# A graph network on one core: in the message pass, the cap goes from GpSimd to VectorE, the product of gate and softplus from VectorE to GpSimd, and scaling and caps one iteration ahead

## The chip, the cores and the metric

The kernel runs on one core of a Trainium2 chip. The metric is the device time of one execution in microseconds. Five engines work side by side from their own instruction queues and meet through semaphores: TensorE (PE in the profile, its weight loads PEld), VectorE (DVE), ScalarE (ACT), GpSimd (POOL) and SyncE (SP), which here issues DMA transfers.

## The reference

Four graph network layers over 6250 nodes of 64 features and 200000 edges sorted by destination, each followed by a residual sum and a layer norm. The change lies in the third layer, in the part that turns every edge's 128 sums into a message of 64 features and sums the messages by destination:

```python
total = jnp.concatenate([atom_fea[dst], atom_fea[src], edge_fea], axis=1)
total = _batchnorm(total @ fc_w.T + fc_b, bn1_w, bn1_b)
gate, core = jnp.split(total, 2, axis=1)
messages = jax.nn.sigmoid(gate) * jax.nn.softplus(core)
aggr = jax.ops.segment_sum(messages, dst, num_segments=N)
```

## The kernel before

The edges are cut into two halves that lie in the lower and the upper 64 partitions, so that a block of 512 columns holds 1024 edges. There are 196 blocks; an iteration handles U = 4 of them, and a pass over the edges has 49 iterations. The kernel has seven passes in turn (SOFT, GCN1, GCN2, STAT, MSG, PNA1, PNA2). The statistics pass (STAT) has left every block's sums in memory (`total_d`, gate part and core part, 512 KB a block) and the scale `bnsc` and bias `bnbi` of the batch norm in columns. The message pass (MSG) reads them back and does the rest. It runs as `message_turns`: iteration after iteration, with a body for even and one for odd iterations (`par` is 0 or 1, and picks one of two sets of four buffers in `totals`, `acts` and `scaled`).

For block u of iteration i the work before the change is:

- SyncE, `message_moves(i)`: `total_load` (L445) brings the sums of block (i, u) into `totals`; it waits until iteration i-2 is through with that buffer, which means the sigmoid of ScalarE (the wait at L442) and GpSimd's two operations. Behind two loads in the same queue stand two stores `rows_store` (L434) of blocks three iterations back, and a small load of the mask (`mask_load`, L423).
- GpSimd, `scale_cores`: `acts` becomes min(core x scale, cap), L655, where the column `bncap` is CAP - bias; `scaled` becomes core x scale + bias, L656. It may be up to two iterations ahead.
- ScalarE, `gates` (sigmoid of the gate part, L1162), `exps` (exp with the bias added, L1170), `logs` (ln(1 + .), L1176), each over two blocks at once, and `rows_out` (L1127), which copies the transposed running sums of iteration i-1 out of PSUM into one of four slots of `obuf`. `rows_out` of a slot waits for the store that last emptied it. Sigmoid needs another function table than exp and ln, so that a table is loaded (L1162 and L1184) twice in every two iterations.
- VectorE, `message_sums`: `softplus` (L1526) is the larger of `acts` and `scaled`, into `msg`; `message` (L1532) multiplies `msg` by the gate; `message_scan` (L1514) is the running sum along the edges, restarted by the mask that TensorE has spread over PSUM (`spread_mask`, L852).
- TensorE, `turn_back` (L827): four transposes of the running sums, for `rows_out`.

The queue of ScalarE is written out by hand in `message_functions`. In the order of its lines, with 0 for blocks 0 and 1, and 2 for blocks 2 and 3, an odd iteration does gates 0, rows_out 0, gates 2, table, exps 0, rows_out 1, exps 2, logs 0, rows_out 2, logs 2, rows_out 3. An even one does exps 0, rows_out 0, exps 2, logs 0, rows_out 1, logs 2, table, gates 0, rows_out 2, gates 2, rows_out 3. The `rows_out` in iteration i are those of iteration i-1. `message_sums` issues softplus 0, message 0, and then for each u softplus u+1, scan u, message u+1.

Of the kernel before, what the change touches and what calls it, by code (L numbers as in the profile page):

```python
# [18 lines left out]
P = 128  # L19
# [4 lines left out]
BLK = P * J  # L24
U = 4
# [68 lines left out]
def gnn_kernel(nc, x, src, dst, ea128, ea16, ea64, W0, b0, W1, b1, W2, b2, fcw, fcb, bn1w, bn1b,  # L94
# [15 lines left out]
    with ctx:  # L110
# [86 lines left out]
        aT = expd  # L197
        stats = feat[:, :, :].rearrange("p w c -> p (w c)")[:, 0:2 * NB * 6].rearrange("p (n k) -> p n k", k=6)
        agg2 = sb("agg2", [P, 2])
        bnsc, bnbi, bncap = sb("bnsc", [P, 2]), sb("bnbi", [P, 2]), sb("bncap", [P, 1])  # L200
        nrow = sb("nrow", [P, 4, F])
        col1 = sb("col1", [P, 4])

# [35 lines left out]
        s_neg = ring("s_neg", one((SOFT, *PNA)))  # L239
        s_eT = ring("s_eT", one((STAT, *PNA)))  # L240
        s_eC = ring("s_eC", one((STAT, *PNA)))
        s_col = ring("s_col", {**one(GATHER), MSG: 2})
        s_zero_out = sem("s_zero_out")
        s_sed = ring("s_sed", one((STAT,), 32))
        s_seT = ring("s_seT", one((STAT,)))
# [1 line left out]
        s_hot = ring("s_hot", one((SOFT,)))  # L247
        s_hus = ring("s_hus", one((SOFT,)))
        s_top = ring("s_top", one((SOFT, MSG)))
        s_arg = ring("s_arg", one((SOFT,)))  # L250
        s_dec = ring("s_dec", one((SOFT, MSG)))
        s_exp = ring("s_exp", {SOFT: 1, MSG: 2})
        s_sg = ring("s_sg", one((MSG,)))
# [86 lines left out]
        def total_here(engine, i, par, u):  # L340

            if par:
                engine.wait_ge(s_sed.sems[u], i * 8 + (8 + s_sed.base[MSG]))
            else:
                engine.wait_ge(s_tot0[u], i * 8 + 16)
# [256 lines left out]
        def _(g):  # L602
# [41 lines left out]
                                             in_offset=bass.IndirectOffsetOnAxis(ap=idx, axis=0))\  # L644
                         .then_inc(s_gat.sems[u], 16)

            def scale_cores(i, par):

                for u in range(U):
                    total_here(g, i, par, u)  # L650
                    if not (isinstance(i, int) and i < 2):
                        s_cus.done(g, MSG, i - 2, u)
                    g.sem_inc(s_in_order, 1)
                    of = totals[:, par * U + u, BLK:]
                    g.tensor_scalar(acts[:, par * U + u, BLK:], of, bnsc[:, 1:2], bncap[:, 0:1], ALU.mult, ALU.min).then_inc(s_col.sems[u], 1)  # L655
                    g.tensor_scalar(scaled[:, par * U + u, :], of, bnsc[:, 1:2], bnbi[:, 1:2], ALU.mult, ALU.add).then_inc(s_col.sems[u], 1)  # L656

            def near_edges():

# [31 lines left out]
            for p in range(7):  # L691
                if p in GCN:
                    x_ = GCN.index(p)
                    if p == GCN1:
                        near_edges()
                    for m in range((MT - ROWS_LAG) * (1 - x_), MT):
                        local_rows(x_, m)
                    joint_rows(x_)
                    continue
                if p == MSG:  # L700
                    g.wait_ge(s_wc, 3)
                    message_turns(g, scale_cores)
                else:
                    if p == STAT:

                        g.wait_ge(s_zero_out, (2 * NB + 1) * 16)
                        for w in range(NT):
                            if w in FIRST_TILES:
                                g.wait_ge(s_tb, ENDS.index(GCN2) * Q + FIRST_TILES.index(w) + 1)
                            g.indirect_dma_start(out=seed_d, out_offset=bass.IndirectOffsetOnAxis(ap=starti[:, w:w + 1], axis=0),  # L710
                                                 in_=feat[:, w, 2 * F:4 * F], in_offset=None,
                                                 bounds_check=2 * H - 1, oob_is_err=False).then_inc(s_sc, 16)
                    if p != SOFT:
                        g.wait_ge(s_td, TABLE[p])
                    if p == STAT:

                        g.wait_ge(s_mi, 16)
                        g.indirect_dma_start(out=mid_row[:, :], out_offset=None, in_=tdst_d,
                                             in_offset=bass.IndirectOffsetOnAxis(ap=mid_i[:, 0:1], axis=0)).then_inc(s_mid, 16)
                    for u in range(U):  # L720
                        rows(p, 0, u)
                    with g.Fori(1, IT) as i:
                        for u in range(U):
                            rows(p, i, u)
                if p == STAT:
                    continue

                g.wait_ge(s_end, 1)
                s_out.all_done(g, p)
                if p > 0:  # L730
                    g.wait_ge(s_free, ENDS.index(p))
                r, k = (runs3_d, 3) if p in RUNS else (runs1_d, 1)
                for w in range(NT):
                    g.indirect_dma_start(out=feat[:, w, F:F + k * F], out_offset=None, in_=r,  # L734
                                         in_offset=bass.IndirectOffsetOnAxis(ap=endi[:, w:w + 1], axis=0))\
                     .then_inc(s_endg[sum(w >= z for _, z in SPAN)], 16)
# [371 lines left out]
        def _(act):  # L1108
# [56 lines left out]
            def exps(i, par, v):  # L1165

                for u in (v, v + 1):
                    s_col.part_done(act, MSG, i, u, 1)
                both = slice(par * U + v, par * U + v + 2)
                A(acts[:, both, BLK:], acts[:, both, BLK:], ACT.Exp, bias=bnbi[:, 1:2]).then_inc(s_exp.sems[v], 1)  # L1170

            def logs(i, par, v):

# [245 lines left out]
        def _(dve):  # L1419
# [105 lines left out]
                s_col.done(dve, MSG, i, u)  # L1525
                TT(msg[:, u, :], acts[:, par * U + u, BLK:], scaled[:, par * U + u, :], ALU.max).then_inc(s_top.sems[u], 1)  # L1526

            def message(i, par, u):

                s_sg.done(dve, MSG, i, u - u % 2)  # L1530
                s_top.done(dve, MSG, i, u)
                TT(msg[:, u, :], msg[:, u, :], acts[:, par * U + u, 0:BLK], ALU.mult).then_inc(s_cus.sems[u], 1)  # L1532

            def message_scan(i, u):

# [5 lines left out]

            def message_sums(i, par):

                softplus(i, par, 0)
                message(i, par, 0)
                for u in range(U):
                    if u + 1 < U:
                        softplus(i, par, u + 1)
                    message_scan(i, u)
                    if u + 1 < U:  # L1550
                        message(i, par, u + 1)

            def running_max(i, u):

# [96 lines left out]
            def edge_pass(p):  # L1651
                link(V.memset(res[:, 1, :, BLK:BLK + 1], 0.0))
                if p in GATHER and p != SOFT:
                    for u in range(U):
                        copy_indices(p, 0, u, u)
                if p == MSG:
                    message_turns(dve, message_sums)
                    return
                if p == SOFT:
                    link(V.memset(top[:, U - 1, BLK:BLK + 1], 0.0))  # L1660
                    s_col.done(dve, SOFT, 0, 0)
                    running_max(0, 0)
                    weights(0, 0)
                for u in range(U):
                    step(p, 0, u, False)
                with dve.Fori(1, IT - 1) as i:
                    for u in range(U):
                        step(p, i, u, False)
                for u in range(U):
                    step(p, IT - 1, u, True)  # L1670
# [408 lines left out]
            link(TT(bnsc[:, :], bnw_c[:, :], col1[:, 0:2], ALU.mult))  # L2079
            link(TT(bnbi[:, :], bnsc[:, :], nrow[:, 0, 0:4:2], ALU.mult))  # L2080
            link(TT(bnbi[:, :], bnb_c[:, :], bnbi[:, :], ALU.subtract))
            link(TS(bncap[:, :], bnbi[:, 1:2], -1.0, CAP, ALU.mult, ALU.add))
            dve.sem_inc(s_wc, 1)


# [113 lines left out]
```

## Time and profile before

| What | us |
|---|---|
| Median of 3 runs | 10464.34 (10455.72 to 10467.83) |
| The profiled execution's own time | 10463.46 |
| Its span in the profile | 10461.7 |
| Message pass, first GpSimd operation to last running sum | 5407.7 to 6037.2 |
| Busy in the whole span: PE, PEld | 5526.5 (53%), 4458.8 (43%) |
| Busy in the whole span: DVE, ACT, POOL | 6467.0 (62%), 2109.5 (20%), 7267.2 (69%) |

Busy times are sums over all seven passes, whose limits differ; the message pass takes some 630 of the 10462 us. The lines quoted further down are of that pass, and times in them count from the start of the span.

### The profile page before, as it was taken

How to read it: one execution, taken by the hardware profiler on the slowest of the kernel's cores; microseconds unless marked ns; L12 is line 12 of the kernel's file. 1: busy time of each engine (PE TensorE's matmuls, PEld its weight loads, DVE VectorE, ACT ScalarE, POOL GpSimd, SP SyncE). 2: the span in 40 equal slices, each digit the busy share in tenths (PEclk: the TensorE clock that was granted, in tenths of full speed). 3: DMA queues.
4: the chain of work that ended last, by engine and by line, in shares of the span. 5: the costliest groups of instructions: out<-in, count | busy, mean ns of one | idle time of the engine just before them, and what ended most of it. 6: DMA issues, size and time to landing. Idle time of an engine off the chain costs nothing.

```text
span 10461.7 us, 124350 instructions
## 1 busy us (share of the span) xinstructions
PE 5526.5 (53%) x33901; PEld 4458.8 (43%) x33999; DVE 6467.0 (62%) x8938; ACT 2109.5 (20%) x2960; POOL 7267.2 (69%) x7048
## 2 busy tenths in 40 slices
PE   4665666548887666666655523333333433333333
PEld 3444444347777445545432223333333333333333
DVE  6777777789932455555568855555555555555556
ACT  1111111137710011111127711111111111111111
POOL 6777777626612777777779947777777577777774
PEclk8777777769998788888865555656565665656556
DMA  8777777624477677777767715555555355555553
GB/s 184 195 195 195 196 196 196 159 83 188 190 282 267 226 238 237 235 239 235 235 209 246 253 49 124 124 125 124 125 123 125 80 124 124 124 124 124 124 124 76
DMA packets 2347313, 1784.12 MB, mean 171 GB/s; under 512 B 1805829, under 2 KB 1977610, under 8 KB 2342282
## 3 DMA queue, kind: packets, MB, share of 16 engines
q1 hardware_dynamic: 828055, 930.52, 27.0%
q10 hardware_dynamic: 1303632, 566.52, 20.3%
q0 software_dynamic: 215456, 284.72, 11.8%
q8 instruction: 119, 1.95, 0.1%
q14 instruction: 51, 0.42, 0.0%
HBM read 921.34 MB, written 861.11 MB: 170 GB/s over the span
## 4 chain that ended last, share of the span: by engine, by line
POOL 57%; issue 23%; DVE 7%; PE 5%; DMA 3%; ACT 2%; SPq 1%; POOLq 0%; ACTq 0%; DVEq 0%
POOL arena L643 53%; PE ph L968 2%; POOL feat L734 1%; POOL sum_d L679 1%; PE pn L968 1%; POOL arena L670 1%; DMA runs_d<-obuf 1%; DVE work L1514 1%; DMA arena<-in_x_dram,idx_src 1%; ACT arena L1170 1%; ACT arena L1176 1%; DVE obuf L1978 0%; PE pn L907 0%; DVE arena L1574 0%; DVE work L1526 0%
## 5 line engine op out<-in xcount | busy, mean ns | idle before, releaser
L643 POOL DMA_INDIRECT arena<-table_d,idx_src x3136 | 2983.0, 951 | 1117.9 <-issue 955.3
L806 PE MATMUL pn<-work,wblk 128*128 128x128 f32 x3136 | 1048.7, 438 | 2412.5 <-DMA arena<-table_d,idx_src 2412.5
L806 PEld LDWEIGHTS pn<-work,wblk 128*128 128x128 f32 x3136 | 837.5, 327 | 2550.8 <-issue 1870.0
L643 POOL DMA_INDIRECT arena<-in_x_dram,idx_src x1568 | 1496.1, 954 | 513.7 <-issue 470.8
L643 POOL DMA_INDIRECT arena<-tsrc_d,idx_src x1568 | 1479.8, 944 | 477.9 <-issue 477.9
L1455 DVE TENSOR_SCALAR idx_src<-src_all 128x8 int32 (+1 forms) x784 | 146.1, 188 | 2350.8 <-PE pn L807 1619.6
L807 PE MATMUL pn<-ident,arena 128*128 128x128 f32 x4704 | 1374.9, 392 | 0.0
L807 PEld LDWEIGHTS pn<-ident,arena 128*128 128x128 f32 x4704 | 1176.2, 306 | 0.0
L1574 DVE STREAM_TRANSPOSE arena<-work 128x512 f32<-128x512 f32 x1568 | 991.1, 679 | 98.0 <-DVE work L1514 98.0
L796 PE MATMUL pn<-work,weT 128*128 128x512 f32 x784 | 554.5, 797 | 660.6 <-DMA arena<-tsrc_d,idx_src 632.7
L1514 DVE TENSOR_TENSOR_SCAN work<-keep,work,pn 128x512 f32<-128x512 bf16 x588 | 752.8, 1280 | 239.9 <-PE ph L819 200.5
L804 PE MATMUL pn<-ident,attr 128*128 128x128 f32 x1568 | 418.7, 360 | 523.9 <-DMA arena<-in_x_dram,idx_src 514.1
L798 PEld LDWEIGHTS pn<-ident,arena 128*128 128x128 f32 x3136 | 510.1, 231 | 265.8 <-issue 265.8
L804 PEld LDWEIGHTS pn<-ident,attr 128*128 128x128 f32 x1568 | 332.0, 259 | 649.1 <-issue 549.1
L1146 ACT ACTIVATE work<-pe_ 128x1024 f32<-128x1024 f32 x196 | 200.9, 1025 | 1786.5 <-PE pe_ L777 1786.5
L1278 ACT ACTIVATE feat<-pn 128x784 bf16<-128x784 f32 x592 | 487.5, 825 | 160.4 <-PE pn L948 152.1
L798 PE MATMUL pn<-ident,arena 128*128 128x128 f32 x3136 | 498.5, 312 | 0.0
L1514 DVE TENSOR_TENSOR_SCAN work<-pe_,work 128x512 f32<-128x512 f32 x392 | 495.7, 1265 | 0.0
L1514 DVE TENSOR_TENSOR_SCAN work<-pos,work,pn 128x512 f32<-128x512 bf16 x392 | 492.0, 1255 | 0.0
L1514 DVE TENSOR_TENSOR_SCAN work<-neg,work,pn 128x512 f32<-128x512 bf16 x392 | 491.7, 1254 | 0.0
L655 POOL TENSOR_SCALAR arena<-feat,bnsc,bncap 128x512 f32<-128x512 f32 x196 | 432.1, 2204 | 55.2 <-DMA feat<-total_d 55.0
L796 PEld LDWEIGHTS pn<-work,weT 128*128 128x128 f32 x784 | 156.0, 248 | 705.6 <-issue 345.4
(404 smaller groups left out, 11025.4 us busy)
## 6 DMA issues: line engine op xcount, KB each, us to landing
runs_d<-arena ACTq DMA_DIRECT2D x2352, 192.0 KB
adj_d<-feat SPq DMA_DIRECT2D x37, 3136.0 KB, 10.6
seed_d<-nothing SPq DMA_DIRECT2D x392, 256.0 KB
arena<-seed_d SPq DMA_DIRECT2D x392, 256.0 KB, 6.8
attr<-in_edge_attr_dram SPq DMA_DIRECT2D x392, 256.0 KB
feat<-total_d SPq DMA_DIRECT2D x196, 512.0 KB, 6.1
keep<-keep_d SPq DMA_DIRECT2D x588, 128.0 KB
feat<-adj_d SPq DMA_DIRECT2D x37, 1600.0 KB, 8.9
```

Source lines behind the costliest of these rows:

```text
L643: g.indirect_dma_start(out=to, out_offset=None, in_=table, in_offset=bass.IndirectOffsetOnAxis(ap=idx, axis=0))\
L655: g.tensor_scalar(acts[:, par * U + u, BLK:], of, bnsc[:, 1:2], bncap[:, 0:1], ALU.mult, ALU.min).then_inc(s_col.sems[u], 1)
L796: mm(to, weT[:, :], eT[:, s, h * BLK:(h + 1) * BLK], start=True, stop=False, skip_group_check=True)
L798: last = mm(to[:, j:BLK:J], gat[:, u, j, h, :], ident[:, :], start=False, stop=True, skip_group_check=True)
L804: mm(to, attr[:, u % 2, j * P:(j + 1) * P], ident[:, :], start=True, stop=False, skip_group_check=True)
L806: mm(to, wblk[:, PNA.index(p), j, :], feat_to[u], start=True, stop=False, skip_group_check=True)
L807: last = mm(to, gat1[:, u, j * P:(j + 1) * P], ident[:, :], start=(p in (GCN1, GCN2)), stop=True, skip_group_check=True)
L968: last = mm(to[:, j * 3 * F:(j + 1) * 3 * F], adj[:, m % 2, j * NT + w, :], tsp[:, w, :], start=(k == 0), stop=(w == NT - 1), skip_group_c ...
L1146: A(eT[:, s, :], pe_[:, :, :].rearrange("p h n -> p (h n)"), ACT.Copy).then_inc(s_eC.sems[u], 1)
L1278: A(adj[:, m % 2, :, g * GROUP:(g + 1) * GROUP].rearrange("p k (b n) -> p k b n", b=2), pn[:, 2 * (k % 2):2 * (k % 2) + 2, 0:4 * KC].rearr ...
L1514: return SCAN(res[:, s, k, 1:BLK + 1], mask, data, res[:, 1 - s, k, BLK:BLK + 1], ALU.mult if mul else ALU.add, ALU.add if mul else ALU.mi ...
L1574: last = V.transpose(to[:, k, :, :], of.rearrange("p (m c) -> p m c", c=SQ))
```

## The change

GpSimd no longer computes the capped product, and the column `bncap` is gone. `scale_core` computes only `scaled` (core x scale + bias), one iteration ahead: in its turn (i, u) GpSimd scales block u of iteration i+1 and then multiplies `msg` of block (i, u) by the gate. VectorE caps `scaled` into `acts` with min(., CAP), also for iteration i+1, in `capped`, right behind `softplus` of (i, u) and ahead of the scan of (i, u-1). ScalarE's exp waits for the cap and adds no bias, since `scaled` holds it. The buffers, the order on ScalarE and the queue of SyncE stay as they are. `s_col` now counts one operation a block, and SyncE's `total_load` waits for that one.

```diff
-        bnsc, bnbi, bncap = sb("bnsc", [P, 2]), sb("bnbi", [P, 2]), sb("bncap", [P, 1])
+        bnsc, bnbi = sb("bnsc", [P, 2]), sb("bnbi", [P, 2])
...
-        s_col = ring("s_col", {**one(GATHER), MSG: 2})
+        s_col = ring("s_col", one((*GATHER, MSG)))
...
-        s_arg = ring("s_arg", one((SOFT,)))
+        s_arg = ring("s_arg", one((SOFT, MSG)))
...
-            def scale_cores(i, par):
+            def scale_core(i, par, u):
+
+                total_here(g, i, par, u)
+                if not (isinstance(i, int) and i < 2):
+                    s_top.done(g, MSG, i - 2, u)
+                g.sem_inc(s_in_order, 1)
+                g.tensor_scalar(scaled[:, par * U + u, :], totals[:, par * U + u, BLK:], bnsc[:, 1:2], bnbi[:, 1:2],
+                                ALU.mult, ALU.add).then_inc(s_col.sems[u], 1)
+
+            def messages(i, par):
 
                 for u in range(U):
-                    total_here(g, i, par, u)
-                    if not (isinstance(i, int) and i < 2):
-                        s_cus.done(g, MSG, i - 2, u)
+                    if not (isinstance(i, int) and i == IT - 1):
+                        scale_core(i + 1, 1 - par, u)
+                    s_sg.done(g, MSG, i, u - u % 2)
+                    s_top.done(g, MSG, i, u)
                     g.sem_inc(s_in_order, 1)
-                    of = totals[:, par * U + u, BLK:]
-                    g.tensor_scalar(acts[:, par * U + u, BLK:], of, bnsc[:, 1:2], bncap[:, 0:1], ALU.mult, ALU.min).then_inc(s_col.sems[u], 1)
-                    g.tensor_scalar(scaled[:, par * U + u, :], of, bnsc[:, 1:2], bnbi[:, 1:2], ALU.mult, ALU.add).then_inc(s_col.sems[u], 1)
+                    g.tensor_tensor(msg[:, u, :], msg[:, u, :], acts[:, par * U + u, 0:BLK], ALU.mult).then_inc(s_cus.sems[u], 1)
...
                     g.wait_ge(s_wc, 3)
-                    message_turns(g, scale_cores)
+                    for u in range(U):
+                        scale_core(0, 0, u)
+                    message_turns(g, messages)
...
                 for u in (v, v + 1):
-                    s_col.part_done(act, MSG, i, u, 1)
+                    s_arg.done(act, MSG, i, u)
                 both = slice(par * U + v, par * U + v + 2)
-                A(acts[:, both, BLK:], acts[:, both, BLK:], ACT.Exp, bias=bnbi[:, 1:2]).then_inc(s_exp.sems[v], 1)
+                A(acts[:, both, BLK:], acts[:, both, BLK:], ACT.Exp).then_inc(s_exp.sems[v], 1)
...
-            def message(i, par, u):
-
-                s_sg.done(dve, MSG, i, u - u % 2)
-                s_top.done(dve, MSG, i, u)
-                TT(msg[:, u, :], msg[:, u, :], acts[:, par * U + u, 0:BLK], ALU.mult).then_inc(s_cus.sems[u], 1)
+            def capped(i, par, u):
+
+                s_col.done(dve, MSG, i, u)
+                TS(acts[:, par * U + u, BLK:], scaled[:, par * U + u, :], CAP, None, ALU.min).then_inc(s_arg.sems[u], 1)
...
             def message_sums(i, par):
 
-                softplus(i, par, 0)
-                message(i, par, 0)
                 for u in range(U):
-                    if u + 1 < U:
-                        softplus(i, par, u + 1)
-                    message_scan(i, u)
-                    if u + 1 < U:
-                        message(i, par, u + 1)
+                    softplus(i, par, u)
+                    if not (isinstance(i, int) and i == IT - 1):
+                        capped(i + 1, 1 - par, u)
+                    if u:
+                        message_scan(i, u - 1)
+                message_scan(i, U - 1)
...
                 if p == MSG:
+                    for u in range(U):
+                        capped(0, 0, u)
                     message_turns(dve, message_sums)
...
-            link(TS(bncap[:, :], bnbi[:, 1:2], -1.0, CAP, ALU.mult, ALU.add))
```

## Rows read from the trace of the kernel before

**Rows 1.** Sum over five 100 us stretches of the message pass: busy us by engine.

```profile
...
sum 500.00, PE 263.71 PEld 131.44 DVE 429.42 ACT 386.01 POOL 482.65; mean PE 52.74 PEld 26.29 DVE 85.88 ACT 77.20 POOL 96.53
...
```

**Rows 2.** Groups by line and shape, 5405 to 6040 us: busy us, mean ns | idle before.

```profile
...
L655 POOL TENSOR_SCALAR arena<-feat,bnsc,bncap 128x512 f32<-128x512 f32 x196 | 432.1, 2204 | 55.2 <-DMA feat<-total_d 55.0 <-issue 0.2
L1514 DVE TENSOR_TENSOR_SCAN work<-pn,work 128x512 f32<-128x512 f32 x196 | 249.9, 1275 | 6.5
...
L1532 DVE TENSOR_TENSOR work<-work,arena 128x512 f32<-128x512 f32 x196 | 175.0, 893 | 7.1 <-ACT arena L1162 5.3
L656 POOL TENSOR_SCALAR feat<-feat,bnsc,bnbi 128x512 f32<-128x512 f32 x196 | 167.2, 853 | 0.0
...
L1526 DVE TENSOR_TENSOR work<-arena,feat 128x512 f32<-128x512 f32 x196 | 141.3, 721 | 89.5 <-ACT arena L1176 89.5
...
```

**Rows 3.** Waits, 5405 to 6040 us: us in total, times, longest us.

```profile
...
DVE work L1526 <- ACT arena L1176: 89.5, 25, 16.3
...
ACT obuf L1127 <- DMA runs_d<-obuf: 83.2, 23, 4.4
...
POOL arena L655 <- DMA feat<-total_d: 55.0, 29, 36.6
...
```

**Rows 4.** Waits of SyncE's DMA queue, the same stretch.

```profile
...
SPq L442 <- ACT arena L1162: 88.3, 24, 14.3
...
```

**Rows 5.** ScalarE's timeline: a table load, and the same one 18 periods on.

```profile
...
5446.12 1.28 ACT L1162 ACT_TABLE_LOAD   x1
...
5900.49 1.28 ACT L1162 ACT_TABLE_LOAD   x1
...
```

**Rows 6.** ScalarE's timeline, one period: start us, us, what [idle before].

```profile
...
5713.30 1.04 ACT L1176 ACTIVATE arena<-arena 128x1024 f32<-128x1024 f32 x1
...
5719.44 0.60 ACT L1127 ACTIVATE obuf<-pn 128x512 f32<-128x512 f32 x1 [2.13 <-PE pn L827]
...
5719.93 1.14 ACT L1170 ACTIVATE arena<-arena,bnbi 128x1024 f32<-128x1024 f32 x1
...
5725.01 1.24 ACT L1162 ACTIVATE arena<-feat,bnbi,bnsc 128x1024 f32<-128x1024 f32 x1
...
5733.19 0.60 ACT L1127 ACTIVATE obuf<-pn 128x512 f32<-128x512 f32 x1 [3.71 <-DMA runs_d<-obuf]
...
5736.23 1.15 ACT L1170 ACTIVATE arena<-arena,bnbi 128x1024 f32<-128x1024 f32 x1
...
5738.80 1.04 ACT L1176 ACTIVATE arena<-arena 128x1024 f32<-128x1024 f32 x1
...
```

**Rows 7.** Chain that ended last, 5698 to 5741 us: start us, us, what.

```profile
...
5714.47 0.70 DVE work L1526
...
5723.71 1.28 ACT L1162
...
5726.64 0.37 SPq L445
...
5727.96 5.20 DMA runs_d<-obuf
...
```

**Rows 8.** Timeline of GpSimd and VectorE in the same period.

```profile
...
5720.64 2.07 POOL L655 TENSOR_SCALAR arena<-feat,bnsc,bncap 128x512 f32<-128x512 f32 x1
5720.85 1.09 DVE L1532 TENSOR_TENSOR work<-work,arena 128x512 f32<-128x512 f32 x1
...
5721.87 0.68 DVE L1526 TENSOR_TENSOR work<-arena,feat 128x512 f32<-128x512 f32 x1
...
5726.08 0.72 DVE L1526 TENSOR_TENSOR work<-arena,feat 128x512 f32<-128x512 f32 x1
...
5726.24 2.50 POOL L655 TENSOR_SCALAR arena<-feat,bnsc,bncap 128x512 f32<-128x512 f32 x1
...
```

**Rows 9.** VectorE groups, by line and shape: one-input float32 operations in SBUF.

```profile
...
L2024 DVE TENSOR_SCALAR arena<-dlo 128x128 f32<-128x128 f32 x74 | 20.4, 275 | 0.0
...
L1907 DVE TENSOR_SCALAR arena<-arena 128x768 f32<-128x768 f32 x3 | 1.7, 560 | 0.1
...
```

## The prediction

> **What bounds the pass now.** I read the busy times of the message pass first, then its groups of instructions, its waits, ScalarE's timeline over one period, and the chain of work that ended last.
>
> By busy time GpSimd is the bound: 482.65 of 500 us, against 429.42 for VectorE and 386.01 for ScalarE [rows 1]. But part of it is waiting inside an instruction: L655 takes 2.07 us undisturbed and 2.20 in the mean, and one that starts 0.16 us after a `softplus` takes 2.50 [rows 2, 8]. And beyond the 36.6 us before the first load, GpSimd idles 55.0 - 36.6 = 18.4 us in 28 waits for loads [rows 3], loads that SyncE holds back until ScalarE has done its `gates` [rows 4]. So another loop closes through GpSimd's supply. The waits show it: VectorE's `softplus` waits for `logs` 25 times, once every two iterations, and `rows_out` waits for its slot's store 23 times, 83.2 us in all, 3.6 us each [rows 3].
>
> Two iterations (8 blocks) take (5900.49 - 5446.12) / 18 = 25.24 us [rows 5]. I call the odd iteration o and the even one after it e. The loop has four legs in the period shown [rows 6, 7]:
>
> - a: `logs` 0 of o ends at 5714.34. VectorE's `softplus` (o,0) starts 0.13 later, then come message, scan and turn_back, until ScalarE's `rows_out` (o,0) at 5719.44, which had waited 2.13 us; right behind it, at 5719.93, starts `exps` 2 of e. 5.59 us.
> - b: from there ScalarE is nearly without a gap to the end of `gates` 0 of e, 5726.25. 6.32 us.
> - c: SyncE, released by these gates, issues two loads (5726.64) and then the store of (o,0) (5727.96), which lands 5.20 us later; `rows_out` (e,0) starts at 5733.19 after a wait of 3.71. 6.94 us.
> - d: ScalarE, without waiting for another engine, to the end of `logs` 0 of the next odd iteration, 5739.84. 6.65 us.
>
> The sum is 25.50, this period's length. The chain of waits runs the same way in this stretch, through the same DMA, `gates`, table load and `softplus` [rows 7]. With the mean period, b + c + d are 25.24 - 5.59 = 19.65 us. The change touches none of these three, so its worth hangs on leg a.
>
> **What the change does, part by part.** I write S for the scaling, M for the product (both on GpSimd), X for `softplus`, C for the cap and N for the scan (on VectorE).
>
> *GpSimd loses L655* (2.07 us a block) and gets M. By busy time that is relief, but GpSimd doesn't stand on the loop, so alone it is worth nothing there.
>
> *VectorE loses `message`* (0.89 us in the mean, 175.0 us in all [rows 2]) and gets C. One-input float32 operations take 275 ns at 128 columns and 560 at 768, 0.445 ns a column, so about 0.45 us at 512 [rows 9]. VectorE has less to do.
>
> *The order on VectorE is the cost.* ScalarE does `exps` 2 of e before `logs` 0, `rows_out` (o,1), `logs` 2 and `gates` 0 of e. Now `exps` 2 of e needs C(e,3), which VectorE issues only behind X(o,3). X(o,0) needs `logs` 0 of o. So leg a becomes: `logs` 0 of o, then X0 C0 X1 C1 N0 X2 C2 N1 X3 C3, then `exps` 2. Before, the caps came from GpSimd, ahead of all this, and leg a held only two X, one message and one scan.
>
> *VectorE and GpSimd hold each other up.* `message`, started 0.21 us after an L655, took 1.09 us instead of 0.66, so it got through 0.64 us after L655's start, and the `softplus` behind it ran its plain 0.68 beside the rest of L655. In the other direction L655 was held 0.43 us behind an X [rows 8]. So I count S as blocking X and C for 0.64 us, X as blocking GpSimd until about 0.1 us before its end, and C likewise. The Trainium skill (SBUF — State Buffer, section Who interferes with whom) says that a VectorE operation with two SBUF inputs and a GpSimd one that reads SBUF exclude each other for the whole instruction; by that L655 would have blocked 2.07 us, and here the trace differs.
>
> *M isn't in the trace.* From below it costs as S, 0.77 us; from above as L655, 2.07 us. It is nearest to S, which reads one operand in 0.64 us; M reads two, so I take 1.30 us, blocking VectorE for 1.20. The Trainium skill (GPSIMD Engine Reference, section 3.1) gives 4497 ns for a float32 tensor_tensor of 2048 columns, of which a quarter is 1.12 us, and its section 4.1 advises against two-input arithmetic on GpSimd; by that estimate leg a would be about 9.7 us and the sum 10558 us instead of 10573.
>
> *Leg a anew.* Times from X0's start; S0 is long done. X0 to 0.68, C0 to 1.05, M0 0.95 to 2.25. X1 is ready at 0.97, is held up until 2.15, ends at 2.83. S1, behind M0 in GpSimd's queue and then held by X1, runs 2.70 to 3.47; C1 waits for it, 3.53 to 3.98. M1 3.88 to 5.18, N0 3.90 to 5.18. X2 5.10 to 5.78, S2 5.65 to 6.42, C2 6.48 to 6.93, M2 and N1 to 8.13. X3 8.05 to 8.73, S3 to 9.37, C3 to 9.88. (An operation on VectorE starts 0.07 us before the last one ends [rows 8].) With 0.13 us in front and some 0.07 behind, leg a is 10.1 us. If M1 gets ahead of C1, which waits for a semaphore while M1 stands next in the queue, C3 ends 0.36 later. I take 10.3, and 10.3 - 5.6 = 4.7 us more a period.
>
> *What else waits.* M of (e,0) also needs `gates` 0 of e, now some 3 us behind X(e,0); GpSimd stands there, and S(o,1) and C(o,1) behind it. Their `exps` 0 comes only after leg c and 3.04 us more (5736.23 - 5733.19 [rows 6]), nearly 10 us after the gates, and C(o,1) is through some 2.6 us after them. Hidden; without that cover the 2.6 us would be on the loop. The loads for S, one iteration earlier than before in GpSimd's order, have been issued over an iteration ahead. `total_load` waits for `s_col` too, which now comes earlier; `gates` remain the last to release it. The one dropped operation on `bncap` is under 0.3 us.
>
> *The ends.* The first four S take 0.77 instead of 2.07 + 0.77 us a block, and the first exps 2 start some 2 us sooner; the last iteration has no S and no C, some 2 us less. 4 us in all.
>
> **The sum.** 24 such legs (the odd iterations of 49) x 4.7 = 113, less 4: 109 us. On the profiled execution's own 10463.46 (1.8 above its span, 0.9 below the median of the runs) this makes 10572.5, so 10573. With M at 0.77 leg a is 8.34 us, +66 - 4, 10526. With M at 2.07 it is 12.35 us, +162 - 4, 10622, and about 10655 if M also gets ahead of C each time (1.3 us more a leg). If nothing contends and S is never late, VectorE's own row of four X, four C and two N is 6.6 us: +24 - 4, 10484.
>
> **Rivals.** About 0.2% (21 us) is what a measurement can tell from no change.
>
> 1. *GpSimd was the bound after all, faster.* For it: 96.5% busy. Then a block costs at least what the two engines need exclusively, 0.64 + 1.20 + 0.60 + 0.35 = 2.8 us, against 3.16 now: (25.24 - 22.3) x 24.5 = 72 us less, 10392. Against it: the loop closes without GpSimd. It decides only if the period falls under 25.24, with b + c + d at 19.65 only if leg a is under 5.6, when VectorE alone needs 6.6. A cheap M (leg a 8.34) together with a store that no longer makes ScalarE wait (3.6 less) would give 24.4, 10440. Chance 0.08.
> 2. *The store stops being waited for.* ScalarE's 3.6 us a period goes and takes up most of the 4.7: 1.1 x 24 - 4 = +22, 10485. Against it: the store is issued behind gates that come later by as much as leg a grows. Chance 0.07.
> 3. *M is cheap, or contention mild.* Leg a 6.6 to 9.0, 10484 to 10541, at the middle 10520. Chance 0.20.
> 4. *M is dear or always first.* 10605 to 10655. Chance 0.13.
>
> My forecast, a leg of 9.0 to 11.6 us and 10541 to 10604, has 0.52. The range of 10490 to 10640 leaves out rival 1, about two thirds of rival 2 and a third of rival 4. Slower by over 0.2%: 0.52 + 0.20 + 0.13 and a little of rival 2, 0.87. Within 0.2%: 0.05. Faster: 0.08.
>
> **What the profile would show.** ScalarE's table loads some 30 us apart instead of 25.24. GpSimd well under 80% busy over the pass, M near 1.3 us, and waits of GpSimd's M for `gates`. `exps` waiting for VectorE's cap, some 4 to 5 us a period, at the place where `rows_out` waited for TensorE. `rows_out` still waiting 3 to 4 us for its store, and `softplus` waiting longer than before for `logs`, about 5 us. Other passes unchanged. I am wrong if C(e,3) isn't the last thing before `exps` 2, or if legs b, c, d shrink.

## The result, and the profile after

The changed kernel takes 10555.42 us (median of 4 runs, 10554.88 to 10572.59) against 10461.84 of the kernel before: 1.0096 times as long, with a 95% interval of 1.0083 to 1.0109, slower by 94 us. 10573 was forecast, with a range of 10490 to 10640.

Each engine's busy time in the message pass, the sum of six stretches of 100 us (compare [rows 1]):

```profile
...
sum 600.00, PE 259.68 PEld 130.38 DVE 450.85 ACT 376.85 POOL 359.14; mean PE 43.28 PEld 21.73 DVE 75.14 ACT 62.81 POOL 59.86
```

GpSimd is busy 59.9% of the time where it was 96.5%, VectorE 75% instead of 86%. No engine is near full, and the pass is longer. The groups from 5400 to 6140 us (busy us, mean ns | idle before; compare [rows 2]):

```profile
...
L664 POOL TENSOR_TENSOR work<-work,arena 128x512 f32<-128x512 f32 x192 | 243.7, 1269 | 294.8 <-ACT arena L1172 136.0 <-DVE work L1536 87.9 <-issue 70.8
L1524 DVE TENSOR_TENSOR_SCAN work<-pn,work 128x512 f32<-128x512 f32 x191 | 243.3, 1274 | 9.5 <-DVE work L1524 9.5
...
L653 POOL TENSOR_SCALAR feat<-feat,bnsc,bnbi 128x512 f32<-128x512 f32 x196 | 202.9, 1035 | 39.4 <-DMA feat<-total_d 39.4
L1541 DVE TENSOR_SCALAR arena<-feat 128x512 f32<-128x512 f32 x196 | 183.6, 937 | 157.0 <-POOL feat L653 157.0
...
```

L664 is the product on GpSimd, L653 the scaling, L1541 the cap, L1536 `softplus`, L1524 the scan. The product takes 1.27 us. The cap takes 0.94 us in the mean, though it needs 0.41: nearly half of the caps are held up. The waits of the pass (compare [rows 3]):

```profile
...
DVE arena L1541 <- POOL feat L653: 157.0, 100, 4.2
ACT arena L1180 <- DVE arena L1541: 155.9, 50, 5.2
POOL work L664 <- ACT arena L1172: 136.0, 24, 5.7
...
ACT obuf L1137 <- DMA runs_d<-obuf: 87.9, 23, 4.8
...
POOL feat L653 <- DMA feat<-total_d: 39.4, 5, 36.3
...
DVE work L1536 <- ACT arena L1186: 28.1, 25, 2.1
...
```

New are the first three: the cap waits for GpSimd's scaling, `exps` (L1180) waits 50 times for the cap, and the product waits 24 times, 5.7 us each, for the `gates`. The store is waited for 23 times as before. `softplus` waits only 28.1 us for the `logs`.

ScalarE's timeline over one period (start us, us, what [idle before]; compare [rows 6]):

```profile
...
5728.35 1.05 ACT L1186 ACTIVATE arena<-arena 128x1024 f32<-128x1024 f32 x1
...
5734.46 1.06 ACT L1180 ACTIVATE arena<-arena 128x1024 f32<-128x1024 f32 x1 [3.15 <-DVE arena L1541]
5736.86 0.60 ACT L1137 ACTIVATE obuf<-pn 128x512 f32<-128x512 f32 x1 [1.34 <-PE pn L837]
5740.50 1.06 ACT L1180 ACTIVATE arena<-arena 128x1024 f32<-128x1024 f32 x1 [3.04 <-DVE arena L1541]
...
5745.25 1.24 ACT L1172 ACTIVATE arena<-feat,bnbi,bnsc 128x1024 f32<-128x1024 f32 x1
...
5753.22 0.60 ACT L1137 ACTIVATE obuf<-pn 128x512 f32<-128x512 f32 x1 [3.50 <-DMA runs_d<-obuf]
...
5758.64 1.04 ACT L1186 ACTIVATE arena<-arena 128x1024 f32<-128x1024 f32 x1
...
```

Leg by leg: `logs` 0 of o ends at 5729.40, and `exps` 2 of e starts at 5740.50 after waiting 3.04 for the cap: leg a is 11.10 us. `gates` 0 of e ends at 5746.49: leg b, 5.99. `rows_out` (e,0) starts at 5753.22, behind its store: leg c, 6.73. `logs` 0 ends at 5759.68: leg d, 6.46. Leg a has doubled, the others stand.

In the table are the mean legs over the whole pass for every kernel of this study, read in the same way from ScalarE's timeline. The period is the distance of the first and last sigmoid table load divided by the periods between them. "Ratio" is the time against the kernel before on the same chip.

| Kernel | a | b | c | d | period | median us | before us | ratio (95%) |
|---|---|---|---|---|---|---|---|---|
| before | 5.65 | 6.15 | 6.85 | 6.65 | 25.17 | 10461.84 | | 1 |
| changed | 11.10 | 5.99 | 7.05 | 6.47 | 30.56 | 10555.42 | 10461.84 | 1.0096 (1.0083 to 1.0109) |
| e1 caps first | 5.73 | 5.98 | 7.18 | 6.47 | 25.26 | 10412.33 | 10445.92 | 0.9963 (0.9949 to 0.9977) |
| e2 stores first | 11.11 | 5.99 | 6.30 | 6.47 | 29.85 | 10520.12 | 10445.92 | 1.0068 (1.0052 to 1.0085) |
| e3 before, stores first | 7.73 | 6.08 | 4.27 | 6.65 | 24.73 | 10451.08 | 10465.18 | 0.9987 (0.9978 to 0.9997) |
| e4 caps and stores first | 5.95 | 5.98 | 5.44 | 6.47 | 23.79 | 10402.41 | 10465.18 | 0.9943 (0.9926 to 0.9959) |
| e5 cap ahead of product | 10.58 | 5.99 | 7.24 | 6.47 | 30.19 | 10526.16 | 10445.92 | 1.0073 (1.0056 to 1.0090) |
| e6 product on VectorE | 8.41 | 5.99 | 7.10 | 6.46 | 27.82 | 10476.31 | 10445.92 | 1.0029 (1.0018 to 1.0039) |
| e7 product alone moved | 14.37 | 6.08 | 7.03 | 6.89 | 34.37 | 10661.58 | 10465.18 | 1.0190 (1.0173 to 1.0207) |
| e8 before, one product | 5.39 | 6.07 | 7.21 | 6.65 | 25.19 | 10454.05 | 10479.98 | 0.9975 (0.9964 to 0.9986) |
| e9 caps, stores first, VectorE | 5.90 | 6.03 | 5.01 | 6.47 | 23.35 | 10406.79 | 10479.98 | 0.9930 (0.9915 to 0.9945) |
| e10 half a product | 8.31 | 5.99 | 6.98 | 6.46 | 27.66 | 10513.81 | 10479.98 | 1.0030 (1.0019 to 1.0040) |
| e11 products of 2 and 3 | 5.90 | 5.98 | 5.43 | 6.47 | 23.71 | 10400.91 | 10462.28 | 0.9941 (0.9925 to 0.9958) |

**Where leg a's time goes.** VectorE's timeline inside that leg, and behind it GpSimd's:

```profile
...
5730.46 1.76 DVE L1536 TENSOR_TENSOR work<-arena,feat 128x512 f32<-128x512 f32 x1
5732.89 1.48 DVE L1541 TENSOR_SCALAR arena<-feat 128x512 f32<-128x512 f32 x1 [0.68 <-POOL feat L653]
...
5737.59 0.66 DVE L1536 TENSOR_TENSOR work<-arena,feat 128x512 f32<-128x512 f32 x1
5738.93 1.48 DVE L1541 TENSOR_SCALAR arena<-feat 128x512 f32<-128x512 f32 x1 [0.68 <-POOL feat L653]
...
```

```profile
...
5730.39 1.27 POOL L664 TENSOR_TENSOR work<-work,arena 128x512 f32<-128x512 f32 x1 [3.63 <-DVE work L1536]
5731.65 1.21 POOL L653 TENSOR_SCALAR feat<-feat,bnsc,bnbi 128x512 f32<-128x512 f32 x1
5732.82 1.26 POOL L664 TENSOR_TENSOR work<-work,arena 128x512 f32<-128x512 f32 x1
...
5737.59 1.31 POOL L653 TENSOR_SCALAR feat<-feat,bnsc,bnbi 128x512 f32<-128x512 f32 x1
5738.86 1.26 POOL L664 TENSOR_TENSOR work<-work,arena 128x512 f32<-128x512 f32 x1
...
5746.74 1.27 POOL L664 TENSOR_TENSOR work<-work,arena 128x512 f32<-128x512 f32 x1 [5.70 <-ACT arena L1172]
...
```

The `softplus` of block 1 at 5730.46 takes 1.76 us, because the product of block 0 (5730.39) has the access. The scaling of block 1 then runs to 5732.86; GpSimd goes on with its next product at 5732.82, and VectorE's cap, which had waited for that scaling, starts at 5732.89 and takes 1.48. The same happens with block 3: scaling to 5738.90, product 5738.86, cap 5738.93 to 5740.41. Of the 196 caps of the pass 96 are that slow: those of blocks 1 and 3 of every iteration but the first, where no product is in the way.

### The profile page after: what moved, and what is told of

Its sections match the earlier page's. It is cut to its first block and busy times, and to the rows that moved or that the text cites. A ratio compares the mean times of both kernels' runs of the same rounds, so it can differ in the third digit from the quotient of the medians.

```text
span 10553.1 us, 124278 instructions
## 1 busy us (share of the span) xinstructions
PE 5533.1 (52%) x33901; PEld 4459.1 (42%) x33999; DVE 6493.2 (62%) x8937; ACT 2103.3 (20%) x2960; POOL 7101.8 (67%) x7048
## 5 line engine op out<-in xcount | busy, mean ns | idle before, releaser
L643 POOL DMA_INDIRECT arena<-table_d,idx_src x3136 | 2959.6, 944 | 1116.5 <-issue 955.2
L643 POOL DMA_INDIRECT arena<-in_x_dram,idx_src x1568 | 1496.3, 954 | 513.4 <-issue 473.9
L643 POOL DMA_INDIRECT arena<-tsrc_d,idx_src x1568 | 1479.8, 944 | 477.9 <-issue 477.9
L1524 DVE TENSOR_TENSOR_SCAN work<-keep,work,pn 128x512 f32<-128x512 bf16 x588 | 752.6, 1280 | 240.8 <-PE ph L829 201.8
L1524 DVE TENSOR_TENSOR_SCAN work<-pe_,work 128x512 f32<-128x512 f32 x392 | 495.7, 1265 | 0.0
L1524 DVE TENSOR_TENSOR_SCAN work<-pos,work,pn 128x512 f32<-128x512 bf16 x392 | 491.8, 1255 | 0.0
L1524 DVE TENSOR_TENSOR_SCAN work<-neg,work,pn 128x512 f32<-128x512 bf16 x392 | 491.5, 1254 | 0.0
L664 POOL TENSOR_TENSOR work<-work,arena 128x512 f32<-128x512 f32 x196 | 248.7, 1269 | 303.0 <-ACT arena L1172 142.6
```

The source lines that it names most:

```text
L643: g.indirect_dma_start(out=to, out_offset=None, in_=table, in_offset=bass.IndirectOffsetOnAxis(ap=idx, axis=0))\
L664: g.tensor_tensor(msg[:, u, :], msg[:, u, :], acts[:, par * U + u, 0:BLK], ALU.mult).then_inc(s_cus.sems[u], 1)
L1524: return SCAN(res[:, s, k, 1:BLK + 1], mask, data, res[:, 1 - s, k, BLK:BLK + 1], ALU.mult if mul else ALU.add, ALU.add if mul else ALU.mi ...
```

## The experiments

All medians, ratios and legs are in the table above.

**e1: the caps first.** From the changed kernel.

```diff
             def messages(i, par):
 
-                for u in range(U):
-                    if not (isinstance(i, int) and i == IT - 1):
+                if not (isinstance(i, int) and i == IT - 1):
+                    for u in range(U):
                         scale_core(i + 1, 1 - par, u)
+                for u in range(U):
...
             def message_sums(i, par):
 
+                if not (isinstance(i, int) and i == IT - 1):
+                    for u in range(U):
+                        capped(i + 1, 1 - par, u)
                 for u in range(U):
                     softplus(i, par, u)
-                    if not (isinstance(i, int) and i == IT - 1):
-                        capped(i + 1, 1 - par, u)
```

> From the changed kernel; GpSimd scales all four blocks of the next iteration before its four products, and VectorE does the four caps ahead of the first softplus, in the time in which it waits for the logs. My theory (the order on VectorE put eight more operations into leg a): leg a falls from 11.1 us to about 5.7, the period from 30.56 to about 25.2, and the kernel takes about 10555 - 129 = 10426 us; exps no longer waits for the cap. Rival (GpSimd and VectorE exclude each other so long, 2.8 us a block, that the order matters little): the period stays above 29 us, 10520 us or more.

Leg a fell to 5.73 us and the period to 25.26. The waits of this kernel over most of the pass no longer hold one of `exps`:

```profile
...
ACT obuf L1138 <- DMA runs_d<-obuf: 83.5, 21, 4.6
...
DVE arena L1542 <- POOL feat L653: 66.1, 84, 2.7
...
```

The instructions are the same ones in another order (on VectorE and on GpSimd, both queues are changed), and 139 us are gone (1.0096 to 0.9963). The rival is out: with the same work on the same two engines a period of 25.3 us is possible. That the ratio is even below 1 doesn't come from the message pass, which takes 626.9 us against 629.5 before. The rest lies behind it: 4397.7 us against 4424.5 before, as in nearly all of these kernels (see the indirect DMAs at the end).

**e2: the stores first.** From the changed kernel, in `message_moves`:

```diff
                 for u in range(0, U, 2):
-                    if not (isinstance(i, int) and i >= IT):
-                        total_load(i, par, u)
-                        total_load(i, par, u + 1)
                     for n in (12, 11):
                         if not (isinstance(i, int) and not 0 <= i * U + u - n < NB):
                             rows_store(i + (u - n) // U, (u - n) % U)
+                    if not (isinstance(i, int) and i >= IT):
+                        total_load(i, par, u)
+                        total_load(i, par, u + 1)
```

> From the changed kernel; SyncE issues the two stores ahead of the two loads, so that they no longer stand behind the gates. If the landing of the store alone sets leg c, the wait of 3.4 us goes: 24 x 3.4 = 82 us less, 10473. My theory: the row copy of (e,0) then waits for TensorE instead, since the product of (e,0) on GpSimd comes only behind the gates and the scan needs the cap of block 1 too; that chain ends 6.2 us behind the gates, against 6.73 with the store, so that 0.5 us a period go, 10543.

ScalarE no longer waits for a store at all, and leg c lost only 0.75 us of its 3.8 us of waiting, for `rows_out` now waits for TensorE:

```profile
...
ACT obuf L1137 <- PE pn L837: 79.7, 36, 3.1
...
```

So the store was the last to arrive, with another chain 0.7 us behind it.

**e3: the same on the kernel before.**

> From the kernel before; SyncE issues the two stores ahead of the two loads. My theory: leg c could shrink by 2.1 us, until the scan of (e,0) ends last, but GpSimd is busy 24.4 of 25.2 us a period and becomes the bound: at most 0.9 us a period less, about 10442. Rival (GpSimd is no bound near this point): 24 x 2.1 = 50 us less, 10412. The indirect DMAs of the passes behind the message pass take 952 ns as in the kernel before, if it is the kind of GpSimd operation in the message pass that made them 8 ns longer than the 944 of the changed kernel.

Leg c fell by 2.6 us, leg a rose by 2.1, the period fell by 0.44, and the ratio is 0.9987. The reason stands in its waits: `exps` (L1170) now waits for GpSimd's L655 (L1127 is `rows_out`):

```profile
...
ACT obuf L1127 <- PE pn L827: 60.2, 44, 1.7
...
ACT arena L1170 <- POOL arena L655: 54.8, 22, 2.6
...
```

GpSimd was a second bound, a small step behind the loop of the four legs.

**e4: caps first and stores first.**

> From the changed kernel; both orders: caps and scaling of the next iteration first, stores ahead of loads. My theory: leg a 5.7, b 6.1, c 3.9 (gates, product on GpSimd, scan, transposes), d 6.5 us: 22.2, or a little more where the transfers or the exclusion of GpSimd and VectorE (22.4) hold it up; some 23 us a period and 10370 us, under both kernels. Rival (GpSimd and VectorE exclude each other for longer): no shorter than with the caps first alone.

The period is 23.79, not 23, and the time beats both kernels. Leg c is 5.44 us instead of 3.9. GpSimd's timeline shows why, and behind it VectorE's:

```profile
...
5705.13 1.27 POOL L665 TENSOR_TENSOR work<-work,arena 128x512 f32<-128x512 f32 x1 [0.71 <-issue]
5706.38 3.70 POOL L653 TENSOR_SCALAR feat<-feat,bnsc,bnbi 128x512 f32<-128x512 f32 x4
...
5717.01 1.26 POOL L665 TENSOR_TENSOR work<-work,arena 128x512 f32<-128x512 f32 x1 [0.71 <-issue]
...
```

```profile
...
5710.11 0.43 DVE L1542 TENSOR_SCALAR arena<-feat 128x512 f32<-128x512 f32 x1 [0.59 <-POOL feat L653]
5710.46 1.28 DVE L1537 TENSOR_TENSOR work<-arena,feat 128x512 f32<-128x512 f32 x2
...
```

The four scalings run only behind the product of block 3 (5705.13). They end at 5710.08, the last cap waits for them, and `softplus` (e,0) comes behind it at 5710.46, when `gates` 0 have already ended (5710.17). From one product of block 3 to the next (5717.01) it is 11.88 us, nearly half of the period, and each step in it is released by the one before. The next turn takes 12.02 us, because a scaling waits 0.26 us for its load. What holds this kernel is this loop through GpSimd's queue rather than that of the four legs.

**e5: the cap ahead of the product.** From the changed kernel, in GpSimd's `messages`:

```diff
                     s_top.done(g, MSG, i, u)
+                    if not (isinstance(i, int) and i == IT - 1):
+                        s_arg.done(g, MSG, i + 1, u)
```

> From the changed kernel; GpSimd's product of block u also waits for VectorE's cap of block u of the next iteration, so that the cap is never behind the product. My theory (each of the two late caps in leg a, of blocks 1 and 3, loses about a product's length): leg a falls from 11.1 to about 10.1, 24 us less, 10531; the cap takes 0.4 us everywhere. Rival (who goes first only shifts the wait): 10555, within 10 us.

Every cap is short now (0.425 us in the mean), but leg a fell by 0.5 us only, half of what I expected. The time went from 1.0096 to 1.0073, and the two intervals overlap: this run doesn't tell the theories apart by time, and by the leg it gives the race 0.5 us. Counted from the end of `logs` 0, the cap of block 1 ends at 4.09 us instead of 4.97, but the cap of block 2 starts at 6.86 instead of 6.66: the gain at block 1 is gone. At the cap of block 3, which ends at 10.47 instead of 11.01, the 0.5 us remain.

**e6: only the caps moved, the product stays on VectorE.** From the changed kernel:

```diff
-                    g.tensor_tensor(msg[:, u, :], msg[:, u, :], acts[:, par * U + u, 0:BLK], ALU.mult).then_inc(s_cus.sems[u], 1)
...
                     if u:
                         message_scan(i, u - 1)
+                    message(i, par, u)
                 message_scan(i, U - 1)
```

> From the changed kernel; the product is back on VectorE (behind the scan of the block before), the scaling and the caps stay one iteration ahead. My theory: leg a is VectorE's own row of four softplus, four caps, three products and two scans, 8.0 us and some 0.5 for GpSimd's scaling, so a period of about 28 us and 10493 us in all: slower than before even with the product where it was. Rival (the product on GpSimd is what costs, the order of the caps is free): about 25.2 us a period, 10430.

Leg a is 8.41 us (8.5 expected), the ratio 1.0029 (10493 / 10462 = 1.0030 expected). The caps in this place make the kernel slower with nothing given to GpSimd; 8.41 - 5.65 = 2.8 of the 5.45 us by which leg a grew are there without the product on GpSimd, the other 2.7 come with it. (By the period the loss is 24 x 2.65 = 64 us. The ratio shows 30, with an interval of 19 to 41. Of the difference 16 us lie behind the pass, which is shorter here, too; the rest I can't place.)

**e7: only the product moved.** The kernel before, with cap and scaling of the next iteration on GpSimd ahead of each product, and no `message` on VectorE.

> From the kernel before; the product goes to GpSimd, the cap stays there too (scaling and cap of the next iteration ahead of each product, exps with the bias). GpSimd has 2.07 + 0.77 + 1.27 = 4.1 us a block: a period of 33 to 35 us, some 10462 + 204 = 10665 us. The indirect DMAs of the later passes: 952 ns if the capped product on GpSimd leaves them slower, 944 if it is the product that makes them faster.

34.37 us a period and a ratio of 1.0190, as expected (10665 / 10462 = 1.0194). This half of the change needs the other.

**e10: half a product.** The changed kernel, where the second half of each block's columns isn't multiplied by the gate:

```diff
-                    g.tensor_tensor(msg[:, u, :], msg[:, u, :], acts[:, par * U + u, 0:BLK], ALU.mult).then_inc(s_cus.sems[u], 1)
+                    g.tensor_tensor(msg[:, u, 0:BLK // 2], msg[:, u, 0:BLK // 2], acts[:, par * U + u, 0:BLK // 2], ALU.mult).then_inc(s_cus.sems[u], 1)
```

> The changed kernel with GpSimd's product over half of each block's columns (the other half of the messages isn't multiplied by the gate): some 0.64 instead of 1.27 us each. My theory: leg a holds three products in a row with VectorE's work (blocks 0, 1 and 3), so it falls by 3 x 0.63 = 1.9 to about 9.2 us, the kernel by 46 us, ratio 1.005. Rival (only VectorE's order counts, contention not): leg a stays at 11.1 us and the ratio at 1.0096.

The product takes 0.74 us, and leg a is 8.31 us: 2.8 us less, where three products a leg give only 1.6. So a product's length counts for more than its own three places in the leg. At blocks 0, 1 and 2 the operations behind it move as well, and block 3's cap no longer meets a product. The ratio is 1.0030, 70 us better.

**e9: caps first, stores first, product on VectorE** in the order of the kernel before (softplus u+1, scan u, message u+1).

> From the kernel with caps first and stores first (period 23.79 us, ratio 0.9943 to before); the product is back on VectorE in the order of the kernel before, GpSimd only scales. If the handover to GpSimd is what lengthened legs a and c there (5.95 and 5.44 us against 5.1 and 3.8 worked out for VectorE alone), the period falls until VectorE's own row is the bound: 8 x (0.60 + 0.37 + 0.59 + 1.19) = 22.0 us, so 22.3 to 22.8 and 24 to 36 us less than there: ratio about 0.991. If VectorE's row of 22 us with its waits costs more than the handover, the period is 23.8 us or more, ratio 0.994 or above.

23.35 us a period and the lowest ratio of the study, 0.9930; its interval overlaps those of e4 and e11. VectorE's busy time:

```profile
...
sum 400.00, PE 227.48 PEld 113.20 DVE 385.25 ACT 325.16 POOL 134.12; mean PE 227.48 PEld 113.20 DVE 385.25 ACT 325.16 POOL 134.12
```

385 of 400 us, while GpSimd has nearly nothing to do (134 us). I read this as VectorE being the bound. That isn't shown, and it is the same reading, of a busy share of 96%, that fails for the kernel before. The chain that ended last passes, in both periods from 5700 to 5750 us, through a load of the sums:

```profile
...
5707.98 6.37 DMA feat<-total_d
...
5731.49 6.21 DMA feat<-total_d
...
```

SyncE issues this load behind the `gates`; GpSimd's scaling, the cap and `softplus` follow it. Such loads are 25.2% of the chain in this stretch. So VectorE and a loop through the loads are both close to the period, and no run here tells which of them sets it.

**e11: GpSimd takes the products of blocks 2 and 3 only.** From e9:

```diff
+                for u in (2, 3):
+                    s_sg.done(g, MSG, i, u - u % 2)
+                    s_top.done(g, MSG, i, u)
+                    g.sem_inc(s_in_order, 1)
+                    g.tensor_tensor(msg[:, u, :], msg[:, u, :], acts[:, par * U + u, 0:BLK], ALU.mult).then_inc(s_cus.sems[u], 1)
...
-                    if u + 1 < U:
-                        message(i, par, u + 1)
+                    if u == 0:
+                        message(i, par, 1)
```

> From the kernel with caps first, stores first and the product back on VectorE (period 23.35 us, VectorE busy 385 of 400 us, ratio 0.9930); GpSimd takes the products of blocks 2 and 3 only, which lie under the scan of the block before and in neither leg. My theory (VectorE's own row bounds that kernel): VectorE loses 4 x 0.59 = 2.4 us a period, the legs (5.2, 6.0, 3.9, 6.5) bound it at 21.6, and with what GpSimd and VectorE hold each other up some 22.3: 25 us less, ratio about 0.9905. Rival (the exclusion of the two engines gives back what VectorE loses): 23.3 us and 0.993.

I was wrong: 23.71 us, not 22.3. VectorE fell to 346 of 400 us busy and nothing was gained. The rival's number came, but GpSimd's timeline and VectorE's show a loop that neither theory had:

```profile
...
5703.90 1.26 POOL L665 TENSOR_TENSOR work<-work,arena 128x512 f32<-128x512 f32 x1 [0.72 <-issue]
5705.15 3.70 POOL L653 TENSOR_SCALAR feat<-feat,bnsc,bnbi 128x512 f32<-128x512 f32 x4
...
5715.79 1.27 POOL L665 TENSOR_TENSOR work<-work,arena 128x512 f32<-128x512 f32 x1 [0.72 <-issue]
...
```

```profile
...
5708.88 0.43 DVE L1542 TENSOR_SCALAR arena<-feat 128x512 f32<-128x512 f32 x1 [0.59 <-POOL feat L653]
5709.22 0.68 DVE L1537 TENSOR_TENSOR work<-arena,feat 128x512 f32<-128x512 f32 x1
...
5714.72 0.90 DVE L1537 TENSOR_TENSOR work<-arena,feat 128x512 f32<-128x512 f32 x1
...
```

The product of block 3 (5703.90) is followed by the four scalings for the next iteration (5705.15, 3.70 us), the last cap waits for the last of them (5708.88), and only behind it comes `softplus` 0 (5709.22) and in the end `softplus` 3 (5714.72), which releases the next product of block 3 at 5715.79. One turn is 11.89 us, two are the period. With the scalings placed ahead of the products as a group, GpSimd's queue order had become a loop of its own. It is the loop of e4, which turns in 11.88 us: that VectorE has two products a turn more to do in e11 and GpSimd two fewer changes its length by 0.01 us.

## Why the prediction was right, point by point

*The bound.* The reading that the pass is held by a loop of four legs, and not by the engine with 96.5% busy, held. e3 shows GpSimd as a second bound just behind, which the prediction had only as a rival: relief of leg c was eaten by a wait for L655.

*The order on VectorE.* This was the step that decided, and it was right: e1 takes the caps (and GpSimd's scalings) out of leg a and the whole loss goes with them, e6 leaves the caps in it, has no product on GpSimd, and is still slower than before.

*The size of leg a: 10.3 us forecast, 11.10 measured.* The product was sized well (1.30 against 1.27 us), and so was the cap (0.45 against 0.41). What I mis-sized is who goes first, and only at one place. From the start of X0 (5729.51) the working has X3 at 8.05 and the end of S3 at 9.37; measured are 8.08 and 9.39. Then the product of block 3 is next in GpSimd's queue and gets ahead of the cap C3, which takes 1.48 us instead of 0.45 and ends at 10.90 instead of 9.88. That is the whole miss: 10.1 + 1.0 = 11.1. The prediction asked the question only at block 1, and priced it at 0.36 us. There the product is ahead, too, every time, but by C2 (6.55, forecast 6.48) nothing is left of it, because S2 then runs right behind that product instead of behind X2. Making the product wait for the cap (e5) gives back 0.5 of the 1.0 us, since the products then start later.

*The other legs.* b, c and d were to stay at 19.65 us together. They are 19.51 by the table. The store's wait is still 3.8 us in 23 cases. e2 says how near rival 2 was: without the wait for the store, a chain through the product and the scan ends 0.7 us earlier, so that at most 17 us (24 x 0.7) were to be had from it.

*The sum.* The period grew by 30.56 - 25.17 = 5.39 us, 24 x 5.39 = 129 us. From the first GpSimd operation to the last scan the pass went from 629.5 to 753.5 us (5400.4 to 6154.0), 124 us more, so the ends gave 5 (4 forecast). I had 109, with 4.7 us a period instead of 5.39. Then 25 us came back where I had expected nothing: everything behind the pass is 4424.5 us before and 4399.1 after. Without this the time would have been about 10580. So that 10573 lies as near to 10555 as it does is in part luck, two errors of opposite sign; the forecast of 10541 to 10604 would have held without it. The part ahead of the pass is 7.3 us shorter, in passes where nothing is changed; runs of one kernel differ by 12 us, and I count it as that. 124 - 25.4 - 7.3 = 91.3, the difference of the two spans.

*The rivals.* Rival 1 (GpSimd the bound, faster) is refuted by the busy shares together with the period. Rival 3, at 9.0 us or less of leg a, didn't come. Rival 4 lies above what was measured, though its mechanism, the product first, was at work.

*What I said the profile would show.* Table loads 30 us apart: 30.56. GpSimd well under 80%: 60%. Waits of the product for the `gates`: 136.0 us. M near 1.3 us: 1.27. C(e,3) the last thing before `exps` 2: yes, with 3.04 us of waiting. `exps` waiting for caps 4 to 5 us a period: 6.2 us (3.15 and 3.04 in the period shown), in two places instead of one. Other passes unchanged: wrong by the 25 us. `softplus` waiting about 5 us for `logs`: wrong, it waits 28.1 us in all, because VectorE itself comes late: GpSimd's product for (e,0) stood behind the gates, and the caps and scans of e behind that.

## What to carry to other kernels

A share of 96% busy doesn't make an engine the bound: follow the chain once around its period, write down its legs, and ask of each moved instruction which leg it enters. An operation for the next round that is put between the operations of this round pays with this round's time, unless its place is one where the engine idles. Once the order is right, it mattered little here which of VectorE and GpSimd does a product: three different divisions (e4, e9, e11) ended within 0.44 us a period of each other, e4 and e11 in the same loop through GpSimd's queue, and the shortest period is that of e9, where GpSimd only scales.

## What the hardware showed that I had not expected

**Later indirect DMAs on GpSimd became 8 ns shorter each.** The groups of GpSimd's indirect DMAs (L643, x3136 in the two passes behind the message pass, x1568 in a pass ahead of it), first of the kernel before, then of the changed one:

```profile
...
L643 POOL DMA_INDIRECT arena<-table_d,idx_src x3136 | 2983.0, 951 | 1117.9 <-issue 955.3 <-DMA table_d<-tab 162.6
...
L643 POOL DMA_INDIRECT arena<-tsrc_d,idx_src x1568 | 1479.8, 944 | 477.9 <-issue 477.9
...
```

```profile
...
L643 POOL DMA_INDIRECT arena<-table_d,idx_src x3136 | 2959.6, 944 | 1116.5 <-issue 955.2 <-DMA table_d<-tab 161.3
...
```

In that pass ahead of the message pass both kernels take 944 ns; behind it the kernel before takes 951 (median 952) and the changed one 944. Those passes wait for these DMAs. By the busy sums it is 23.4 us, about the 25.4 us above. Of the experiments, only e3, which keeps the kernel before's GpSimd work, has 951 behind the pass; there the part behind the pass takes 4421.6 us, in all the others 4397.7 to 4408.2, and every ratio of the table but e3's contains this gain. e1, e4, e7 and e11, all with a product on GpSimd, have 943 or 944. The others have 946 on both sides of the pass, whether they have a product on GpSimd (e2, e5, e10) or neither it nor the capped product L655 (e6, e9), so that a product isn't what tells 944 from 946. So I tried the kernel before with one more instruction behind its last scaling:

**e8: one product**, with a 128x1 buffer for it.

```diff
                     message_turns(g, scale_cores)
+                    g.tensor_tensor(last_one[:, :], valid[:, :], valid[:, :], ALU.mult)
```

> The kernel before with one more GpSimd instruction, a product of two 128x1 columns behind its last scaling of the message pass. The changed kernel's indirect DMAs on GpSimd in the two later passes took 944 ns, those of the kernel before 952 (3136 of them, 25 us), and the kernel with cap, scaling and product on GpSimd 944. If a product as the last kind of GpSimd operation ahead of those passes is what makes them shorter, they take 944 ns here and the kernel 25 us less than before, 0.24%. If it is the mix during the pass, they stay at 952 and the time stays within 0.1%.

GpSimd's groups of e8:

```profile
...
L644 POOL DMA_INDIRECT arena<-table_d,idx_src x3136 | 2958.9, 944 | 1118.0 <-issue 955.2 <-DMA table_d<-tab 162.8
...
L704 POOL TENSOR_TENSOR last_one<-valid 128x1 f32<-128x1 f32 x1 | 0.2, 188 | 0.0
...
```

The indirect DMAs take 944 ns, the part behind the pass 4400.0 us, and the kernel is 0.25% faster (0.9964 to 0.9986), for one instruction of 188 ns. That this instruction takes the 7 ns away is shown. The cause is open: whether it must be a product, or any instruction would do, or only a shift of GpSimd's program behind it, wasn't tried, and the two kernels with 951 ns have one and the same GpSimd program.

**GpSimd's capped product (L655) holds VectorE for part of its time, its product (L664) for nearly all of it.** A `softplus` that meets a product at 5730.46 ends at 5732.22, 0.56 us after the product (5731.66), most of its own length. Behind L655 in the kernel before it was only the first 0.64 of 2.07 us [rows 8]. The Trainium skill (SBUF — State Buffer, section Who interferes with whom) has the whole instruction; the product agrees with that, L655 doesn't. For the product's price the Trainium skill (GPSIMD Engine Reference, section 3.1) has 4497 ns at 2048 columns; a quarter of it, 1.12 us, is an estimate for 512, and 1.27 us were measured.
